# Twelve of 36 probability blocks per turn: transposed by VectorE and DMA in place of TensorE

## The chip, the cores and the metric

One Trainium2 chip, one core of it. The metric is the device time of one execution in microseconds (us). TensorE is PE in the profile, its weight loads PEld, VectorE is DVE, ScalarE is ACT, GpSimd is POOL, and SyncE, which issues most DMAs, is SP.

## The reference

One transformer block with two modulated layer norms. Batch 2, 1024 rows, 256 columns; 16 heads in 4 groups, each group with its own keys and values, head size 128.

```python
h = _layernorm(x) * (1 + ca) + sa
qkv = einsum('bsh,ph->bsp', h, weight_qkv)          # q: 4 heads, k: 1, v: 1, for each of 4 groups
scores = einsum('bsgqd,btgd->bgqst', q, k) * scale  # causal
attn = softmax(scores, axis=-1)
out = einsum('bgqst,btgd->bsgqd', attn, v)
x = x + ga * (out @ weight_proj.T)
h = _layernorm(x) * (1 + cb) + sb
x = x + gb * ffn(h)     # Hadamard transforms folded in, silu(gate) * up, down
```

## The kernel before

All products are made in three matmuls of split operands: a value is rounded to a high part (name ending in `_hi`) and the remainder is kept as a low part (`_lo`); `three` (L797) multiplies high by high, high by low and low by high.

The attention runs in 8 **turns**, one for each pair of batch and group. A turn first makes q, k and v (the steps "C" and "VT"), then goes over the 8 row blocks of 128 queries, from the last (row 7, 1024 keys) to the first (row 0, 128 keys). For row `i` and head `h` the step "S" makes the scores on PE (L903 to L909), DVE adds the mask and takes the row's maximum (L702), ACT takes the exponential and the row's sum (L487), and POOL inverts the sum and scales the row (L373, L378) into `prob`, in place. `prob` has two slots, so that the scores of row i-1 are made while row i is used.

A probability block (i, j) is 128 queries by 128 keys for 4 heads, so 128 x 512 numbers. There are 36 in a turn, numbered n = 0 to 35 in the order of `UNITS`: row 7 has n = 0 to 7, row 6 n = 8 to 14, row 5 n = 15 to 20, row 4 n = 21 to 25. Each must stand transposed for the product with v. The step "T" does so: PE transposes the 4 heads' 128 x 128 squares into one of two PSUM banks (L924, 4 matmuls against the identity), ACT copies the bank to `pt_hi` (L506), DVE subtracts to `pt_lo` (L706). The step "V" then multiplies block n by its v block (three matmuls of 512 columns) into the row's PSUM sum; it stands two blocks behind "T". When a row's last V is done, ACT and DVE split the row's output (`o_hi`, `o_lo`), and the step "Y" multiplies it by the projection weights (12 matmuls of 256 columns).

One list, `WALK`, made by `walk()` and written out by hand rules (`SCORES_AT` says after which block the next row's four S steps stand), sets the order of the steps of a turn. PE, ACT and DVE each go through this list and issue their own part of a step; all four engines run their instructions strictly in their written order, with semaphores between them. POOL has the four normalisations of each row in order of the rows, and after row 6 (`if s == 1`) it splits the next turn's q/k/v weights: `w_hi` (L331) and `w_lo` (L386). SP loads these weights from HBM, one load of `wp_raw` and one of `w_raw` a turn (L290, L294).

After the turns come the FFN's weight transforms and the FFN itself; the change touches them only in that the down weights `raw_down` and their sums and differences (`sum_dn`, `dif_dn`) are loaded and made at another time.

Of the kernel before, what the change touches and what calls it, by code (L numbers as in the profile page):

```python
# [5 lines left out]
F32 = mybir.dt.float32  # L6
F32R = mybir.dt.float32r
# [23 lines left out]
LAST = {i: max(n for n, u in enumerate(UNITS) if u[0] == i) for i in STEPS}  # L31

# [10 lines left out]
def walk():  # L43
# [24 lines left out]
    return out  # L68
# [21 lines left out]
def build(nc, x_in, wqkv, wproj, wmod, c_cols, wug, wdn, su_ug, su_dp, ws_ug, ws_dp, ident_in, mask_in, had_in, out):  # L90
    ctx = ExitStack()
    with ctx:
# [17 lines left out]
        pt_hi = sb("pt_hi", [P, 3, CH], F32R)  # L110
        pt_lo = sb("pt_lo", [P, 3, CH], F32R)
# [8 lines left out]
        raw_down = sb("raw_down", [P, NM * HID])  # L120
        sum_dn, dif_dn = (sb(name, [P, 2, KH, HID])[:, :, :, :] for name in ("sum_down", "dif_down"))
# [42 lines left out]
        raw_dn = raw_down[:, :].rearrange("p (a k o n) -> p a k o n", a=2, k=KH, o=2)  # L164
# [41 lines left out]
        pv_done, oh_done, ol_done = sem("pv_done"), sem("o_hi_done"), sem("o_lo_done")  # L206
        y_done, add_done = sem("y_done"), sem("x_added")
# [12 lines left out]
        PER_PE = {qkv_done: 12, vtr_done: 2, s_done: 32, t_done: NU, pv_done: NU, y_done: NT}  # L220
        PER_ACT = {qkv_hi: 10, vt_done: 2, v_hi_s: 2, exp_done: 32, pth_done: NU, oh_done: NT}
        PER_DVE = {qkv_lo: 10, v_lo_s: 2, max_done: 32, ptl_done: NU, ol_done: NT, add_done: NT}
        PER_POOL = {prob_done: 32, rinv_done: 32}
# [9 lines left out]
        CHUNKS += [("q", h, 1) for h in range(QPG)] + [("q", h, 0) for h in range(QPG)]  # L233

# [30 lines left out]
        def _(sp):  # L265
# [18 lines left out]
            sp.dma_start(raw_down[:, :], wdn).then_inc(raw_s[4], 16)  # L284
# [12 lines left out]
            wide = sum(i + 1 for i in STEPS if i >= CT)  # L297
# [10 lines left out]
        def _(pool):  # L308
# [39 lines left out]
            pool.wait_ge(raw_s[4], 16)  # L348
            a = raw_dn
            g_.tensor_tensor(sum_dn, a[:, :, :, 0, :], a[:, :, :, 1, :], ALU.add)  # L350
            g_.tensor_tensor(dif_dn, a[:, :, :, 0, :], a[:, :, :, 1, :], ALU.subtract).then_inc(fly_s, 1)
            pool.wait_ge(gate_ok, 1)
            for b in range(B):
                for g in range(NKV):
# [13 lines left out]
                    for s, i in enumerate(STEPS):  # L368
                        for h in range(QPG):
                            e = QPG * s + h  # L370

                            pool.wait_ge(exp_done, this(exp_done, t, e + 1))
                            g_.tensor_tensor(rinv[:, s % 2, h:h + 1], rsum[:, s % 2, h:h + 1], mone[:, :],  # L373
                                             ALU.pow).then_inc(rinv_done, 1)
                            pool.wait_ge(rinv_done, this(rinv_done, t, e + 1))
                            pool.sem_inc(pool_gate, 1)
                            row = prob[:, s % 2, h, 0:(i + 1) * P]
                            g_.tensor_scalar(row, row, rinv[:, s % 2, h:h + 1], 1.0, ALU.mult, ALU.mult).then_inc(prob_done, 1)  # L378
                        if s == 1:
# [7 lines left out]
                                             ALU.subtract).then_inc(w_ready, 1)  # L387

# [29 lines left out]
        def _(act):  # L418
# [37 lines left out]
            for b in range(B):  # L456
                for g in range(NKV):
# [34 lines left out]
                    for what, n, h in WALK:  # L492
# [72 lines left out]
        def _(dve):  # L565
# [96 lines left out]
            for b in range(B):  # L662
                for g in range(NKV):
# [21 lines left out]
                    for what, n, h in WALK:  # L685
# [390 lines left out]
```

## Time and profile before

| | |
|---|---|
| median of 3 runs | 979.47 us (979.19 to 979.89) |
| the profiled execution | 979.04 us |
| its span, first to last instruction | 977.2 us |
| mean granted TensorE clock | 0.997 |
| PE busy | 947.1 us |
| DVE busy | 653.1 us |
| ACT busy | 516.6 us |
| POOL busy | 467.7 us |

The span is shorter than the profiled execution's own time by 1.8 us. Busy times are of a single execution; matmuls are pipelined and their ends are modelled, so two starts in a row tell more of PE's pace than a duration does. A line number is that of the kernel before.

### The profile page before, as it was taken

The numbers are of one execution on the slowest core, as the hardware profiler recorded it, in microseconds if no ns is written. First come the engines' busy times: TensorE is split into PE (matmuls) and PEld (weight loads), VectorE is DVE, ScalarE is ACT, GpSimd is POOL, SyncE is SP. The second block draws the span as 40 slices with busy tenths as digits, with TensorE's granted clock in tenths as the row PEclk, the third lists the DMA queues.
The fourth block names the chain that finished last, engine by engine and source line by source line (L and its number), as shares of the span: only waits on it lengthen the run. The fifth ranks groups of instructions, "written<-read, shape, count | busy, mean of one in ns | idle before, by whom it ended". The sixth has DMA issues, their size and how long they took to land.

```text
span 977.2 us, 14506 instructions
## 1 busy us (share of the span) xinstructions
PE 947.1 (97%) x5344; PEld 816.0 (83%) x5344; DVE 653.1 (67%) x1290; ACT 516.6 (53%) x1085; POOL 467.7 (48%) x603
## 2 busy tenths in 40 slices
PE   6899999999999999999999999999999999999997
PEld 5688888888898889888988898889888987888885
DVE  6777657775777577757775777567757776864553
ACT  2466646664666466646664666466646665331221
POOL 3665646564556455545654565456545656120000
PEclk9999999999999999999999999999999999999999
DMA  8000000100010001000000010001000020000000
GB/s 313 24 1 33 2 22 1 33 1 22 1 33 2 22 1 33 1 23 1 33 1 22 1 33 1 22 1 34 1 1 1 1 87 1 1 8 15 21 21 21
DMA packets 9666, 21.92 MB, mean 22 GB/s; under 512 B 1280, under 2 KB 5504, under 8 KB 9472
## 3 DMA queue, kind: packets, MB, share of 16 engines
q1 hardware_dynamic: 8736, 20.45, 6.2%
q8 instruction: 40, 0.66, 0.3%
q10 hardware_dynamic: 864, 0.60, 0.2%
q14 instruction: 26, 0.21, 0.1%
HBM read 18.96 MB, written 2.10 MB: 22 GB/s over the span
## 4 chain that ended last, share of the span: by engine, by line
PE 80%; DVE 9%; ACT 5%; POOL 3%; issue 2%; DMA 1%; SPq 0%; DVEq 0%; POOLq 0%; ACTq 0%
PE ps L801 17%; PE ps L803 16%; PE ps L802 16%; PE ps L924 10%; PE ps L903 6%; PE ps L909 6%; PE ps L906 6%; ACT prob L487 2%; POOL rinv L373 2%; DVE pt_lo L706 2%; POOL prob L378 2%; DVE xhat L614 1%; DVE ps L702 1%; PE ps L825 1%; DVE v_lo L681 1%
## 5 line engine op out<-in xcount | busy, mean ns | idle before, releaser
L706 DVE TENSOR_TENSOR pt_lo<-ps,pt_hi 128x512 fp32r<-128x512 f32 x288 | 198.0, 690 | 101.7 <-ACT pt_hi L506 98.9
L506 ACT ACTIVATE pt_hi<-ps 128x512 fp32r<-128x512 f32 x288 | 171.0, 597 | 134.1 <-PE ps L924 132.6
L373 POOL TENSOR_TENSOR rinv<-rsum,mone 128x1 f32<-128x1 f32 x256 | 140.7, 550 | 211.5 <-ACT prob L487 210.7
L378 POOL TENSOR_SCALAR prob<-prob,rinv 128x1024 f32<-128x1024 f32 (+7 forms) x256 | 192.2, 751 | 53.3 <-POOL rinv L373 53.3
L487 ACT ACTIVATE prob<-ps,nmax 128x1024 f32<-128x1024 f32 (+7 forms) x256 | 189.5, 741 | 50.0 <-DVE nmax L702 48.3
L702 DVE CUSTOM_DVE_ANT_0 ps<-ps,mask_f 128x1024 f32<-128x1024 f32 (+7 forms) x256 | 192.9, 765 | 21.8 <-PE ps L909 19.5
L924 PE MATMUL ps<-ident,prob 128*128 128x128 f32 x1152 | 175.1, 273 | 6.2 <-DVE pt_lo L706 3.6
L924 PEld LDWEIGHTS ps<-ident,prob 128*128 128x128 f32 x1152 | 140.3, 140 | 36.8 <-DVE pt_lo L706 10.9
L801 PE MATMUL ps<-pt_hi,v_hi 128*128 128x512 f32 x288 | 132.5, 460 | 1.3 <-DVE pt_lo L706 0.5
L803 PE MATMUL ps<-pt_hi,v_lo 128*128 128x512 f32 x320 | 126.3, 395 | 0.0
L903 PE MATMUL ps<-k_hi,q_hi 128*128 128x512 f32 (+4 forms) x384 | 117.6, 360 | 0.0
L802 PE MATMUL ps<-pt_lo,v_hi 128*128 128x512 f32 x288 | 113.5, 394 | 0.0
L909 PE MATMUL ps<-k_hi,q_lo 128*128 128x512 f32 (+4 forms) x384 | 110.8, 343 | 0.0
L906 PE MATMUL ps<-k_lo,q_hi 128*128 128x512 f32 (+4 forms) x384 | 110.5, 342 | 0.0
L801 PE MATMUL ps<-h_hi,w_hi 128*128 128x512 f32 x192 | 76.1, 396 | 0.3 <-POOL h_lo L327 0.3
L906 PEld LDWEIGHTS ps<-k_lo,q_hi 128*128 128x128 f32 x384 | 71.0, 189 | 5.9
L903 PEld LDWEIGHTS ps<-k_hi,q_hi 128*128 128x128 f32 x384 | 68.1, 189 | 9.1
L802 PE MATMUL ps<-h_lo,w_hi 128*128 128x512 f32 x192 | 75.1, 391 | 0.0
L803 PE MATMUL ps<-h_hi,w_lo 128*128 128x512 f32 x192 | 75.0, 391 | 0.0
L909 PEld LDWEIGHTS ps<-k_hi,q_lo 128*128 128x128 f32 x384 | 70.7, 189 | 4.9
L801 PE MATMUL ps<-wp_hi,o_hi 128*128 128x256 f32 x256 | 73.8, 288 | 0.0
L803 PE MATMUL ps<-wp_hi,o_lo 128*128 128x256 f32 x256 | 72.2, 282 | 0.0
(134 smaller groups left out, 1575.8 us busy)
## 6 DMA issues: line engine op xcount, KB each, us to landing
w_raw<-in_wqkv SPq DMA_DIRECT2D x9, 768.0 KB, 4.2
wp_raw<-in_wproj SPq DMA_DIRECT2D x8, 512.0 KB, 3.5
x<-in_x SPq DMA_DIRECT2D x4, 512.0 KB, 9.8
prob<-in_wug SPq DMA_DIRECT2D x4, 512.0 KB, 5.3
out_y<-prob SPq DMA_DIRECT2D x4, 512.0 KB, 3.0
prob<-in_wmod SPq DMA_DIRECT2D x1, 1024.0 KB, 9.7
raw_down<-in_wdn SPq DMA_DIRECT2D x1, 1024.0 KB, 14.1
prob<-in_wmod SPq DMA_DIRECT2D x1, 512.0 KB, 5.2
```

The lines of the kernel that those rows point to most:

```text
L378: g_.tensor_scalar(row, row, rinv[:, s % 2, h:h + 1], 1.0, ALU.mult, ALU.mult).then_inc(prob_done, 1)
L487: a_.activation(prob[:, s % 2, h, 0:nb * w].rearrange("p (a n) -> p a n", a=nb), score_banks(i, h).rearrange("p (a n) -> p a n", a=nb)[:, ...
L506: a_.activation(pt_hi[:, n % 3, :], T[n % 2], ACT.Copy).then_inc(pth_done, 1)
L702: v_.tensor_tensor_reduce(row, row, late, -1.0, 3.0e38, ALU.add, ALU.min, nmax[:, s % 2, h:h + 1]).then_inc(max_done, 1)
L706: v_.tensor_tensor(pt_lo[:, n % 3, :], T[n % 2], pt_hi[:, n % 3, :].bitcast(F32), ALU.subtract).then_inc(ptl_done, 1)
L801: mm(dst, w_h, r_h, start=start, stop=False)
L802: mm(dst, w_h, r_l, start=False, stop=False)
L803: return mm(dst, w_l, r_h, start=False, stop=stop)
L903: mm(dst[:, a * CH:a * CH + wide], q_hi[:, h, q_at], k_hi[:, a * w:a * w + wide], start=True, stop=False)
L906: mm(dst[:, a * CH:a * CH + wide], q_hi[:, h, q_at], k_lo[:, a * w:a * w + wide], start=False, stop=False)
L909: last = mm(dst[:, a * CH:a * CH + wide], q_lo[:, h, q_at], k_hi[:, a * w:a * w + wide], start=False, stop=True)
L924: last = tr(T[n % 2][:, h * P:(h + 1) * P], prob[:, s % 2, h, j * P:(j + 1) * P], ident[:, :])
```

## The change

Blocks (i, j) with i in 7, 6, 5 and j among the row's last four leave PE: n = 4 to 7, 11 to 14 and 17 to 20, twelve of 36 ("swapped"; the other 24 are "turned").

For these, a new step "X" (row, head) has DVE transpose the 128 x 512 piece of `prob` in 32 x 32 squares into the buffer `blocks`, one instruction a head, four a row. When all four heads of a row are there, SP issues 16 transfers from SBUF to SBUF, each 32 partitions by 512 numbers, that put the squares in their places in one half of `swapped`. `blocks` is single: the next row's first X waits until these transfers have landed. X stands in the order where a count of assumed costs, begun at the step S, has reached 3300 (`BEHIND`).

The step "E" takes the place of "T" for these blocks: ACT copies the block from `swapped` to `pt_hi`, and POOL, not DVE, subtracts to `pt_lo`. PE has nothing to do in it. V then waits for POOL's semaphore.

POOL now goes through `WALK` too, for its S and E parts. The split of the next turn's weights moves from behind row 6's normalisations to behind the last one of row 4 (`WEIGHTS_AFTER = 4`). `pt_hi` and `pt_lo` get a fourth buffer. `raw_down` shares its space with `swapped`, and `sum_dn` and `dif_dn` with `blocks`, so that load and these two POOL operations move from the start of the program to the last turn.

```diff
+SWAP_ROWS = [7, 6, 5]
+GROUP = 4
+SWAPPED = [n for n, (i, j) in enumerate(UNITS) if i in SWAP_ROWS and j > i - GROUP]
+TURNED = [n for n in range(NU) if n not in SWAPPED]
...
+BEHIND = 3300
+WEIGHTS_AFTER = 4
+
+def with_blocks(walk):
+    cost = {"C": 1360, "VT": 900, "L": 1000, "T": 443, "V": 680, "Y": 1400, "E": 0}
+    out, open_blocks, now = [], [], 0
+    for what, n, h in walk:
+        while open_blocks and now >= open_blocks[0][0]:
+            out.append(open_blocks.pop(0)[1])
+        out.append((what, n, h))
+        now += 160 * (n + 1) if what == "S" else cost[what]
+        if what == "S" and n in SWAP_ROWS:
+            open_blocks.append((now + BEHIND, ("X", n, h)))
+    return out + [block for _, block in open_blocks]
...
+                    for r, i in enumerate(SWAP_ROWS):
+                        at = group(t, i)
+                        sp.wait_ge(block_done, this(block_done, t, QPG * (r + 1)))
+                        if at >= 2:
+                            sp.wait_ge(el_done, len(SWAPPED) + (at - 1) * GROUP)
+                        for kb in range(NB):
+                            for a in range(NB):
+                                sp.dma_start(swapped[kb * QB:(kb + 1) * QB, at % 2, a * GROUP * P:(a + 1) * GROUP * P],
+                                             blocks[a * QB:(a + 1) * QB, kb * GROUP * P:(kb + 1) * GROUP * P]).then_inc(swap_s[at % 2], 16)
...
+                    def swapped_low(n):
+                        pool.wait_ge(eh_done, this(eh_done, t, SWAPPED.index(n) + 1))
+                        g_.tensor_tensor(by_head(pt_lo, n), swapped_tile(t, n), by_head(pt_hi, n).bitcast(F32),
+                                         ALU.subtract).then_inc(el_done, 1)
+
+                    for what, i, h in WALK:
+                        if what == "E":
+                            swapped_low(i)
+                        if what == "S":
+                            normalise(i, h)
+                        if what == "S" and (i, h) == (WEIGHTS_AFTER, QPG - 1):
...
                             split_w()
...
+                        if t == TURNS - 1 and what == "S" and (i, h) == (2, QPG - 1):
+                            pool.wait_ge(raw_s[4], 16)
+                            g_.tensor_tensor(sum_dn, a[:, :, :, 0, :], a[:, :, :, 1, :], ALU.add)
+                            g_.tensor_tensor(dif_dn, a[:, :, :, 0, :], a[:, :, :, 1, :], ALU.subtract).then_inc(fly_s, 1)
...
+                        if what == "E":
+                            i, j = UNITS[n]
+                            if n >= 4:
+                                act.wait_ge(pv_done, this(pv_done, t, n - 3))
+                            if j == i - GROUP + 1:
+                                act.wait_ge(*landed(group(t, i)))
+                            a_.activation(by_head(pt_hi, n), swapped_tile(t, n), ACT.Copy).then_inc(eh_done, 1)
+                            exps()
...
+                        if what == "X":
+                            s = NT - 1 - n
+                            at = group(t, n)
+                            if h == 0 and at:
+                                dve.wait_ge(*landed(at - 1))
+                            dve.wait_ge(prob_done, this(prob_done, t, QPG * s + h + 1))
+                            v_.transpose(blocks[:, :].rearrange("p (k j h q) -> p j k h q", k=NB, j=GROUP, h=QPG)[:, :, :, h, :],
+                                         prob[:, s % 2, h, (n + 1 - GROUP) * P:(n + 1) * P].rearrange(
+                                             "p (j k q) -> p j k q", j=GROUP, k=NB)).then_inc(block_done, 1)
...
+                            if n in SWAPPED:
+                                pe.wait_ge(el_done, this(el_done, t, SWAPPED.index(n) + 1))
+                            else:
+                                pe.wait_ge(ptl_done, this(ptl_done, t, turned(n) + 1))
```

How it moves the order, at three places. The first is **DVE in the first turn, around row 6's scores**: the `pt_lo` of n = 1 to n = 3, with the maxima (two rows each, `ps,nmax` and `nmax`) of scores (6,1), (6,2) and (6,3). Before:

```order
L706 TENSOR_TENSOR pt_lo<-ps,pt_hi 128x512 [waits pt_hi_done]
L702 ISA ps,nmax<-ps,mask_f 128x2x448 [waits scores_done]
L702 ISA nmax 128x1
L706 TENSOR_TENSOR pt_lo<-ps,pt_hi 128x512 [waits pt_hi_done] x3
L702 ISA ps,nmax<-ps,mask_f 128x2x448 [waits scores_done]
L702 ISA nmax 128x1
```

Now:

```order
L795 TENSOR_TENSOR pt_lo<-ps,pt_hi 128x512 [waits pt_hi_done]
L803 STREAM_TRANSPOSE blocks<-prob 128x4x4x32 [waits prob_done,blocks_swapped0]
L791 ISA ps,nmax<-ps,mask_f 128x2x448 [waits scores_done]
L791 ISA nmax 128x1
L795 TENSOR_TENSOR pt_lo<-ps,pt_hi 128x512 [waits pt_hi_done] x2
L803 STREAM_TRANSPOSE blocks<-prob 128x4x4x32 [waits prob_done]
L791 ISA ps,nmax<-ps,mask_f 128x2x448 [waits scores_done]
L791 ISA nmax 128x1
```

The first of these transposes is X (6,0). It waits for row 7's transfers, and it stands ahead of the maximum of (6,2) and of the low parts of n = 2 and 3. The low part of n = 4 is gone from DVE.

The second place is **POOL in the first turn, behind the third normalisation of row 4**. Before, the weights' split stands behind row 6's last normalisation:

```order
L373 TENSOR_TENSOR rinv<-rsum,mone 128x1 [waits exp_done]
L378 TENSOR_SCALAR prob<-prob,rinv 128x896 [waits rinv_done]
L331 TENSOR_SCALAR w_hi<-w_raw 128x1536 [waits w_raw_loaded,qkv_done]
L386 TENSOR_TENSOR w_lo<-w_raw,w_hi 128x1536 [waits pool_self]
L373 TENSOR_TENSOR rinv<-rsum,mone 128x1 [waits exp_done]
```

Now it stands behind row 4's last, among the low parts of row 5:

```order
L448 TENSOR_TENSOR pt_lo<-swapped,pt_hi 128x512 [waits swapped_hi_done]
L438 TENSOR_TENSOR rinv<-rsum,mone 128x1 [waits exp_done]
L443 TENSOR_SCALAR prob<-prob,rinv 128x640 [waits rinv_done]
L398 TENSOR_SCALAR w_hi<-w_raw 128x1536 [waits w_raw_loaded,qkv_done]
L463 TENSOR_TENSOR w_lo<-w_raw,w_hi 128x1536 [waits pool_self]
L448 TENSOR_TENSOR pt_lo<-swapped,pt_hi 128x512 [waits swapped_hi_done] x3
```

The first `pt_lo` is that of n = 17, the three at the end are those of n = 18, 19 and 20; between them stand the normalisation of (4,3) and the whole split.

The third place is **SP in the first turn**. It issued two weight loads a turn; now 48 transfers follow them:

```order
L345 DMA wp_raw<-in_wproj 128x1024 [waits wp_ready]
L349 DMA w_raw<-in_wqkv 128x1536 [waits w_ready]
L359 DMA swapped<-blocks 32x512 [waits blocks_turned]
L359 DMA swapped<-blocks 32x512 x15
L359 DMA swapped<-blocks 32x512 [waits blocks_turned]
L359 DMA swapped<-blocks 32x512 x15
```

## Rows read from the trace of the kernel before

**Rows 1.** The page: busy time, share of the span and instructions of each engine.

```profile
PE 947.1 (97%) x5344; PEld 816.0 (83%) x5344; DVE 653.1 (67%) x1290; ACT 516.6 (53%) x1085; POOL 467.7 (48%) x603
```

**Rows 2.** Groups of instructions: busy us, mean ns of one, idle before.

```profile
L706 DVE TENSOR_TENSOR pt_lo<-ps,pt_hi 128x512 fp32r<-128x512 f32 x288 | 198.0, 690 | 101.7 <-ACT pt_hi L506 98.9
L924 PE MATMUL ps<-ident,prob 128*128 128x128 f32 x1152 | 175.1, 273 | 6.2 <-DVE pt_lo L706 3.6 <-POOL prob L378 2.3
L506 ACT ACTIVATE pt_hi<-ps 128x512 fp32r<-128x512 f32 x288 | 171.0, 597 | 134.1 <-PE ps L924 132.6
...
L386 POOL TENSOR_TENSOR w_lo<-w_raw,w_hi 128x1536 fp32r<-128x1536 f32 x8 | 28.1, 3507 | 0.7
...
L327 POOL TENSOR_TENSOR h_lo<-h,h_hi 128x512 fp32r<-128x512 f32 x14 | 18.2, 1301 | 39.5 <-ACT h_hi L446 23.6 <-DVE h_hi L622 15.8
...
L331 POOL TENSOR_SCALAR w_hi<-w_raw 128x1536 fp32r<-128x1536 f32 x9 | 13.3, 1482 | 1.3 <-DMA w_raw<-in_wqkv 1.3
```

**Rows 3.** Timeline of PE, second turn: start, duration, instruction, idle before.

```profile
174.70 0.28 PE L801 MATMUL ps<-wp_hi,o_hi 128*128 128x256 f32 x1
...
176.14 0.60 PE L924 MATMUL ps<-ident,prob 128*128 128x128 f32 x4
...
177.28 0.60 PE L924 MATMUL ps<-ident,prob 128*128 128x128 f32 x4
...
193.13 0.40 PE L801 MATMUL ps<-pt_hi,v_hi 128*128 128x512 f32 x1
...
193.83 0.60 PE L924 MATMUL ps<-ident,prob 128*128 128x128 f32 x4
```

**Rows 4.** Timeline of POOL, DVE and ACT, second turn: (6,3) is normalised, (4,3) too.

```profile
162.22 1.09 DVE L702 CUSTOM_DVE_ANT_0 ps<-ps,mask_f 128x896 f32<-128x896 f32 x1
...
163.71 1.00 ACT L487 ACTIVATE prob<-ps,nmax 128x896 f32<-128x896 f32 x1
...
164.89 0.55 POOL L373 TENSOR_TENSOR rinv<-rsum,mone 128x1 f32<-128x1 f32 x1 [2.42 <-ACT prob L487]
...
165.64 1.02 POOL L378 TENSOR_SCALAR prob<-prob,rinv 128x896 f32<-128x896 f32 x1 [0.20 <-POOL rinv L373]
...
189.32 0.80 POOL L378 TENSOR_SCALAR prob<-prob,rinv 128x640 f32<-128x640 f32 x1 [0.21 <-POOL rinv L373]
```

**Rows 5.** Timeline of PE, second turn: the steps at which the three places begin and end.

```profile
165.98 0.51 PE L903 MATMUL ps<-k_hi,q_hi 128*128 128x384 f32 x2
...
167.03 0.60 PE L924 MATMUL ps<-ident,prob 128*128 128x128 f32 x4
...
179.55 0.45 PE L903 MATMUL ps<-k_hi,q_hi 128*128 128x320 f32 x2
...
186.47 0.60 PE L924 MATMUL ps<-ident,prob 128*128 128x128 f32 x4
...
191.31 0.39 PE L903 MATMUL ps<-k_hi,q_hi 128*128 128x512 f32 x1
```

**Rows 6.** Timeline of SP's queue, then DMA issues with the us from issue to landing.

```profile
137.60 0.33 SPq L290 DMA_DIRECT2D wp_raw<-in_wproj  x1
...
793.57 2.59 SPq L300 DMA_DIRECT2D prob<-in_wug  x4
...
wp_raw<-in_wproj SPq DMA_DIRECT2D x8, 512.0 KB, 3.5
...
sc<-in_c SPq DMA_DIRECT2D x1, 2.0 KB, 1.7
```

**Rows 7.** Timeline of DVE, second turn: maximum of (6,0) ends, low part of n = 1.

```profile
153.76 0.14 DVE L702 DVE_READ_ACCUMULATOR2_ANT nmax<- 128x1 f32 x1
...
157.61 0.69 DVE L706 TENSOR_TENSOR pt_lo<-ps,pt_hi 128x512 fp32r<-128x512 f32 x1
```

**Rows 8.** PE's longest wait in a turn; stages with busy us and granted clock (PEclk).

```profile
37.86 0.63 PE L825 MATMUL ps<-ident,xhat 128*128 128x128 f32 x4 [3.72 <-DVE xhat L614]
...
38.60:42.00 3.40, 3.40 (x9) 2.63 (x9) 1.18 (x2) 1.93 (x4) 3.32 (x3) 0.50 0.01 2
```

More of the change, by code:

```diff
@@ L67, in walk @@
     out += [("V", NU - 3, 0), ("V", NU - 2, 0), ("T", NU - 1, 0), ("Y", 2, 0), ("V", NU - 1, 0), ("Y", 1, 0), ("Y", 0, 0)]
-    return out
+    return with_blocks([("E", n, 0) if what == "T" and n in SWAPPED else (what, n, h) for what, n, h in out])
+BEHIND = 3300
[11 more added lines that the diff above has]
+    return out + [block for _, block in open_blocks]
 WALK = walk()
@@ L109, in build @@
         prob = sb("prob", [P, 2, QPG, SEQ])
-        pt_hi = sb("pt_hi", [P, 3, CH], F32R)
-        pt_lo = sb("pt_lo", [P, 3, CH], F32R)
+        pt_hi = sb("pt_hi", [P, 4, CH], F32R)
+        pt_lo = sb("pt_lo", [P, 4, CH], F32R)
+        blocks = sb("blocks", [P, GROUP * CH])
+        swapped = sb("swapped", [P, 2, GROUP * CH])
+        raw_down = swapped[:, 0, :]
+        sum_dn, dif_dn = (blocks[:, n * 4 * HID:(n + 1) * 4 * HID].rearrange("p (a k n) -> p a k n", a=2, k=KH)
+                          for n in range(2))
         o_hi = sb("o_hi", [P, 2, CH], F32R)
@@ L206, in build @@
         pv_done, oh_done, ol_done = sem("pv_done"), sem("o_hi_done"), sem("o_lo_done")
+        block_done, swap_s = sem("blocks_turned"), [sem(f"blocks_swapped{n}") for n in range(2)]
+        eh_done, el_done = sem("swapped_hi_done"), sem("swapped_lo_done")
         y_done, add_done = sem("y_done"), sem("x_added")
@@ L295, in _ @@
                                  wqkv[bass.ds(g + 1, 1), :, :].rearrange("a p (k n) -> p (a k) n", k=KH)).then_inc(wraw_s, 16)
-            wide = sum(i + 1 for i in STEPS if i >= CT)
+                    for r, i in enumerate(SWAP_ROWS):
[7 more added lines that the diff above has]
+                                             blocks[a * QB:(a + 1) * QB, kb * GROUP * P:(kb + 1) * GROUP * P]).then_inc(swap_s[at % 2], 16)
+            sp.wait_ge(el_done, (TURNS + 1) * len(SWAPPED))
+            sp.dma_start(raw_down, wdn).then_inc(raw_s[4], 16)
+            wide = len([n for n in TURNED if UNITS[n][0] >= CT])
             sp.wait_ge(t_done, this(t_done, TURNS - 1, wide))
@@ L367, in _, with normalise @@
                     ln_low(1, b, g, 0)
[L368 to L379, printed above, removed]
+                    def normalise(i, h):
+                        s = NT - 1 - i
+                        e = QPG * s + h
+                        pool.wait_ge(exp_done, this(exp_done, t, e + 1))
+                        g_.tensor_tensor(rinv[:, s % 2, h:h + 1], rsum[:, s % 2, h:h + 1], mone[:, :],
+                                         ALU.pow).then_inc(rinv_done, 1)
+                        pool.wait_ge(rinv_done, this(rinv_done, t, e + 1))
+                        pool.sem_inc(pool_gate, 1)
+                        row = prob[:, s % 2, h, 0:(i + 1) * P]
+                        g_.tensor_scalar(row, row, rinv[:, s % 2, h:h + 1], 1.0, ALU.mult, ALU.mult).then_inc(prob_done, 1)
+                    def swapped_low(n):
[8 more added lines that the diff above has]
+                        if what == "S" and (i, h) == (WEIGHTS_AFTER, QPG - 1):
                             pool.wait_ge(wraw_s, (t + 2) * 16)
```

53 lines of the change are left out of this document (31 added, 22 removed).

## The prediction

> **What bounds the kernel now.** I read the page first: PE is busy for 947.1 of 977.2 us, the next engine, DVE, for 653.1 [rows 1]. PE sets the time, and its waits are small: in front of its 1152 transposes it idled 6.2 us in all [rows 2]. Then I read PE's starts, since durations overlap. Y, T and T follow at 174.70, 176.14 and 177.28 [rows 3]: a Y takes 1.44 us, and a T with the V behind it 1.14 us. A V without a T in front takes 0.70 us, from 193.13 to 193.83 [rows 3]. So a T costs PE 0.44 us, part of it in the matmul behind it. Third come the chains from a score to its normalised row and from there to a low part, since the change puts V behind them [rows 4, 7].
>
> **What is removed.** 12 T in each of 8 turns: 96 x 0.44 = 42 us of PE's time, 5.3 us a turn. This is the whole gain, and it needs PE to find its operands ready.
>
> **What is added off PE.** DVE loses 12 low parts a turn (690 ns) and gets 12 transposes of the same 128x512. No row shows such a transpose; I take 0.7 us by the nearest, the low part itself [rows 2], and twice that as the far end, nothing below. ACT's copy now reads SBUF and stays at 0.6 us. Neither engine is full. POOL gets 12 low parts a turn, 1.30 us each by the `h_lo` of the same size [rows 2]. On its sum of 467.7 us that is 125 us more [rows 1], which fits; its place in the order does not. PE without T's consumes a V each 0.70 us, POOL makes a low part each 1.3 us, and POOL runs strictly in order, so that each low part stands behind the normalisation and the split written ahead of it.
>
> The fourth buffer costs nothing. The later load of `raw_down`, and its two POOL operations behind row 2 of the last turn, lie beside PE's rows 2 to 0; if that cover fails they cost two 1.3 to 3.5 us operations once [rows 2]. SP's two weight loads are not late behind the transfers: they are wanted only a turn later.
>
> **The transfers.** SP's steady issue takes 0.33 us, four other loads in a row took 2.59 us, so 0.65 each [rows 6]. A landing takes 1.7 us for 2 KB and 3.5 us for 512 KB. The transfers of a row are 16, of 64 KB. I take 15 x 0.33 + 2.0 = **7.0 us** from DVE's last transpose of a row to the landing (the short issue, since a transfer has 32 lines). Ends: 4 us, if issue hardly counts and the 1 MB moves like the 512 KB load; 15 x 0.65 + 3.5 = 13 us. The Trainium skill, page "DMA: Bandwidth & Descriptors", section "Anatomy of one DMA — SWDGE (gpsimd) path", gives for another issue path 2.0 us fixed plus the bytes at 436 GB/s. As an estimate by that page one 1 MB transfer would take 4.4 us, and the sum below would come to about 1115. No run here shows a transfer from SBUF to SBUF.
>
> **Place 1, row 7's swapped blocks (second turn's clock).** The last transpose of row 7 starts when DVE is done with the maximum of (6,0), at 153.90 [rows 7], ends at 154.6, and the data land at 161.6. DVE reaches X (6,0) at 158.3, behind the low part of n = 1 [rows 7], and waits until 161.6. Behind it are queued: X itself (162.3), the maximum of (6,2), 1.15 us (163.45), the low part of n = 2 (164.15). ACT's exponential of (6,2) then ends at 164.6, the copy of n = 3 at 165.2; DVE: low part of n = 3 at 165.9, X (6,1) 166.6, maximum of (6,3) 167.75. ACT ends its exponential at 168.9, POOL the inversion and scaling (164.89 to 166.66, so 1.8 us [rows 4]) at 170.7, and the low part of n = 5, which stands behind it, at 172.0. V of n = 5 starts then and ends at 172.7. Before, the step behind it started at 165.98 [rows 5]. Loss 6.7 us, with the four T already out.
>
> **Place 2, row 6.** From 172.7: S (5,0) 1.2 to its end by the starts of [rows 5] and the tail of the last matmul, maximum 1.0, X (6,3) 0.7, at 175.65; landing at 182.65; X (5,0) 183.35; the low part of row 7's output, queued behind it, 184.05; Y of row 7 (1.44) ends 185.5, having waited 2.9. DVE meanwhile: low part of n = 10 at 184.75, X (5,1) 185.45, maximum of (5,3) 186.45; exponential 187.5, normalisation 189.2, low part of n = 11 190.5, of n = 12 191.8. V of n = 12 ends at 192.5; before, S (4,0) started at 179.55 [rows 5]. Loss 12.95 in all, so 6.3 here.
>
> **Place 3, row 5 and the weights.** From S (4,0) to the end of S (4,3) took 6.92 us [rows 5], now 0.44 less: 199.0. Scaling of (4,3) ended 3.65 us behind that point (186.47 to 190.12 [rows 4, 5]); POOL, which first has the low part of n = 17, comes to 203.65. Then the split: 1.48 + 3.51 + a gap, 5.06 us [rows 2], to 208.7, and the low part of n = 18 at 210.0. PE's work in between is V 16, Y, V 17, 2.84 us. V of n = 18 ends at 210.7, after a wait of 7 us; before, 191.31 [rows 5]. Loss 19.4 in all, so 6.4 here. Behind it POOL's low parts of n = 19 and 20 keep pace with the S steps between.
>
> **The clock.** After PE's wait of 3.72 us the granted clock was 0.50 (1.2 GHz) for 3.4 us of full work [rows 8], which loses 1.7 us. Two waits a turn are longer than that one. Behind n = 18 I count 1.7, behind n = 11 only 1.1, since the V of n = 12 waits 0.6 anyway: 2.8 us a turn. The Trainium skill, page "TensorE: Matmul & The Clock Gate", section "Part 1: The HAM clock gate", says that the throttled state is the default and activity lifts it; by that, the trace agrees. Without it the sum would be 22 us less, 1134.
>
> **Sum.** 8 x (6.7 + 6.3 + 6.4 + 2.8) = 8 x 22.2 = 178. Against the profiled execution's own time, 979.04 + 178 = **1157 us**; it stands 0.4 below the median of the runs, which is nothing here. A microsecond of landing time moves places 1 and 2 by one each, 16 us in the sum.
>
> **Rivals.**
> 1. *The transfers are quick, POOL alone is in the way.* With nothing lost on DVE: POOL's chain from (6,3) makes n = 5 late by 1.7 us net, n = 12 by 1.4, n = 18 by 5.9 (190.12 + 5.06 + 1.30 + 0.70 = 197.2 against 191.31). 8 x 9.0 = 72, so 1051. With a landing of 3.7 us and the transposes still queued on DVE, 1157 - 16 x 3.3 = 1104. For it: transfers of a free queue. Against: 16 issues. Chance 0.22.
> 2. *Faster.* The low parts are ready whenever PE comes, and the 42 us are kept: 979 - 42 = 937. It decides at n = 18: S to low part must take less than PE's 2.84 us, where the rows add to 10.0 (3.65 + 5.06 + 1.30). For it speaks only that POOL, ACT and DVE all have idle time; chance 0.03.
> 3. *The transfers are slow.* Landing 13 us: 1157 + 16 x 6 = 1253, for it the 0.65 us issue. Chance 0.10.
> 4. *The matmuls that leave are hidden anyway, nothing waits*: about 979. The starts show T on PE's own path [rows 3], so 0.01.
>
> The Trainium skill, page "VectorE: DVE Perf Modes", section "Rules for kernel authors", advises TensorE for 128x128 transposes where a PSUM destination will do; it gives no time for a mix as here, and it points the way of my forecast.
>
> **How the numbers follow.** My forecast, a time set by all three places, has 0.64; with landing 4 to 10 us it runs from 1109 to 1205, a transpose of twice the time adds some 10. The range 1080 to 1215 takes that and the upper half of rival 1, and leaves out its lower half, rivals 2, 3 and 4: 0.2 or a little more. A measurement of this kernel tells 0.2% from no change. Faster 0.03, same 0.01, slower 0.96.
>
> **What would show it.** In the changed kernel's profile: PE's busy time lower but waits in front of Y and the V matmuls of some 25 us a turn, the longest, about 7 us, on POOL's `pt_lo` and eight times; DVE's transposes of X (6,0) and X (5,0) waiting some 3 us each on a DMA; a granted clock well under 0.997; turns some 22 us longer. Wrong would be: landing far from 7 us, the wait at n = 18 under 5 us, or low parts far from 1.3 us.

## The result and the profile after

The changed kernel takes **1258.59 us** (median of 4 runs, 1257.09 to 1261.66) against 979.33 us of the kernel before (4 runs, 978.55 to 979.89): 1.2856 times as long, 95% interval 1.283 to 1.2882. The forecast was 1157 us with a range of 1080 to 1215. The direction was right, the time lies 44 us above the range, at rival 3 (1253 us).

The page of the changed kernel: the busy line, two of its groups and two of its DMA issues.

```profile
PE 993.4 (79%) x4960; PEld 827.5 (66%) x4960; DVE 639.0 (51%) x1290; ACT 514.5 (41%) x1085; POOL 585.8 (47%) x699
...
L803 DVE STREAM_TRANSPOSE blocks<-prob 128x512 f32<-128x512 f32 x96 | 67.7, 705 | 137.3 <-DMA swapped<-blocks 125.9
...
L448 POOL TENSOR_TENSOR pt_lo<-swapped,pt_hi 128x512 fp32r<-128x512 f32 x96 | 119.6, 1271 | 0.0
...
swapped<-blocks SPq DMA_DIRECT2D x384, 64.0 KB, 2.0
...
wp_raw<-in_wproj SPq DMA_DIRECT2D x8, 512.0 KB, 3.8
```

PE has 384 transposes fewer and is yet busy for 46 us longer than before [rows 1], at a mean granted clock of 0.875. DVE's transpose takes 0.705 us (0.7 taken), POOL's low part 1.27 us (1.30 taken), and a single transfer lands in 2.0 us (as taken). None of the new operations is dearer than in the sum. What they wait for is: PE's largest waits, then those of DVE and of ACT on the transfers (us in total, times, the longest).

```profile
PE ps L899 <- POOL pt_lo L448: 118.2, 41, 6.7
PE ps L899 <- DVE pt_lo L795: 61.8, 13, 8.3
PE ps L899 <- DVE o_lo L809: 55.3, 8, 7.4
...
DVE blocks L803 <- DMA swapped<-blocks: 125.9, 16, 8.6
...
ACT pt_hi L595 <- DMA swapped<-blocks: 71.2, 16, 6.9
```

DVE's 16 waits are two a turn, of 7.9 us each, where about 3 was expected. One turn (the fourth), from its timelines: SP's queue behind row 7's last transpose; DVE's last transpose of row 7, and the first of row 6 and of row 5; PE's seven waits.

```profile
452.91 10.01 SPq L359 DMA_DIRECT2D swapped<-blocks  x16
```

```profile
452.18 0.71 DVE L803 STREAM_TRANSPOSE blocks<-prob 128x512 f32<-128x512 f32 x1
...
464.35 0.71 DVE L803 STREAM_TRANSPOSE blocks<-prob 128x512 f32<-128x512 f32 x1 [7.63 <-DMA swapped<-blocks]
...
490.93 0.71 DVE L803 STREAM_TRANSPOSE blocks<-prob 128x512 f32<-128x512 f32 x1 [8.26 <-DMA swapped<-blocks]
```

```profile
466.71 0.80 PE L899 MATMUL ps<-pt_hi,v_hi 128*128 128x512 f32 x1 [7.35 <-DVE pt_lo L795]
470.38 0.79 PE L899 MATMUL ps<-pt_hi,v_hi 128*128 128x512 f32 x1 [0.23 <-POOL pt_lo L448]
474.36 0.79 PE L899 MATMUL ps<-pt_hi,v_hi 128*128 128x512 f32 x1 [2.34 <-POOL pt_lo L448]
492.37 0.55 PE L899 MATMUL ps<-wp_hi,o_hi 128*128 128x256 f32 x1 [7.36 <-DVE o_lo L809]
498.40 0.79 PE L899 MATMUL ps<-pt_hi,v_hi 128*128 128x512 f32 x1 [1.85 <-POOL pt_lo L448]
513.72 0.50 PE L899 MATMUL ps<-pt_hi,v_hi 128*128 128x512 f32 x1 [3.74 <-POOL pt_lo L448]
521.39 0.79 PE L899 MATMUL ps<-pt_hi,v_hi 128*128 128x512 f32 x1 [6.71 <-POOL pt_lo L448]
```

The 16 issues of one row take 10.01 us, 0.63 each, not 0.33. DVE's transpose ends at 452.89 and the next one can start at 464.35: **the landing is 11.5 us behind, not 7.0**. It is so in most turns; in some rows one of the 16 issues is long (up to 1.57 us), and the landing is then up to 12.4 us behind. Everything that stands behind the waiting transpose on DVE comes late: the low part of n = 2 (PE waits 7.35 at 466.71, place 1) and the low part of row 7's output (7.36 at 492.37, in front of Y, place 2). At 521.39 stands the wait for the low part of n = 18, place 3, 6.71 us where 7 was forecast. The POOL timeline in front of it shows the split of the weights in its way, as forecast:

```profile
513.63 0.54 POOL L438 TENSOR_TENSOR rinv<-rsum,mone 128x1 f32<-128x1 f32 x1
514.38 0.80 POOL L443 TENSOR_SCALAR prob<-prob,rinv 128x640 f32<-128x640 f32 x1 [0.21 <-POOL rinv L438]
515.14 1.47 POOL L398 TENSOR_SCALAR w_hi<-w_raw 128x1536 fp32r<-128x1536 f32 x1
516.70 3.42 POOL L463 TENSOR_TENSOR w_lo<-w_raw,w_hi 128x1536 fp32r<-128x1536 f32 x1
520.08 3.72 POOL L448 TENSOR_TENSOR pt_lo<-swapped,pt_hi 128x512 fp32r<-128x512 f32 x3
```

The table of windows of the same turn (PE busy, PEld, DVE, ACT, POOL, granted clock, DMA share, GB/s) shows the clock at its lower level behind each of the long waits:

```profile
458.00:464.00 6.00, 1.36 (x7) 0.91 (x5) 0.00 (x0) 0.00 (x0) 1.02 (x1) 0.98 0.43 105
464.00:476.00 12.00, 6.58 (x13) 3.84 (x14) 5.23 (x9) 4.76 (x9) 7.28 (x8) 0.50 0.00 0
...
488.00:500.00 12.00, 5.78 (x19) 4.59 (x20) 5.12 (x9) 3.29 (x6) 4.34 (x5) 0.50 0.14 34
...
516.00:524.00 8.00, 2.61 (x6) 2.04 (x7) 0.00 (x0) 0.00 (x0) 7.71 (x5) 0.50 0.30 100
```

In the row 458 to 464 PE, DVE and ACT all stand nearly still while the transfers run at 105 GB/s.

### The profile page after: what moved, and what is told of

It reads as the page before. It is cut to its first block, busy times and chain, and to the rows that moved or that the text cites. A ratio compares the mean times of both kernels' runs of the same rounds, so it can differ in the third digit from the quotient of the medians.

```text
span 1255.3 us, 14290 instructions
## 1 busy us (share of the span) xinstructions
PE 993.4 (79%) x4960; PEld 827.5 (66%) x4960; DVE 639.0 (51%) x1290; ACT 514.5 (41%) x1085; POOL 585.8 (47%) x699
## 4 chain that ended last, share of the span: by engine, by line
PE 43%; SPq 17%; DVE 12%; POOL 12%; ACT 6%; DMA 4%; issue 4%; POOLq 0%; DVEq 0%; ACTq 0%
SPq L359 17%; PE ps L899 11%; PE ps L901 10%; PE ps L900 10%; DMA swapped<-blocks 4%; POOL prob L443 4%; DVE ps L791 3%; PE ps L1023 3%; ACT prob L568 3%; PE ps L1001 3%; DVE blocks L803 3%; PE ps L1004 3%; PE ps L1007 3%; POOL rinv L438 3%; POOL pt_lo L448 2%
## 5 line engine op out<-in xcount | busy, mean ns | idle before, releaser
L899 PE MATMUL ps<-pt_hi,v_hi 128*128 128x512 f32 x288 | 149.6, 519 | 181.8 <-POOL pt_lo L448 118.2
L587 ACT ACTIVATE pt_hi<-ps 128x512 fp32r<-128x512 f32 x192 | 114.4, 596 | 245.2 <-PE ps L1023 243.7
L899 PEld LDWEIGHTS ps<-pt_hi,v_hi 128*128 128x128 f32 x288 | 61.9, 215 | 223.0 <-POOL pt_lo L448 144.1
L795 DVE TENSOR_TENSOR pt_lo<-ps,pt_hi 128x512 fp32r<-128x512 f32 x192 | 132.0, 688 | 76.4 <-ACT pt_hi L587 75.5
L803 DVE STREAM_TRANSPOSE blocks<-prob 128x512 f32<-128x512 f32 x96 | 67.7, 705 | 137.3 <-DMA swapped<-blocks 125.9
L1023 PE MATMUL ps<-ident,prob 128*128 128x128 f32 x768 | 123.7, 284 | 4.7 <-POOL prob L443 4.3
L448 POOL TENSOR_TENSOR pt_lo<-swapped,pt_hi 128x512 fp32r<-128x512 f32 x96 | 119.6, 1271 | 0.0
L1023 PEld LDWEIGHTS ps<-ident,prob 128*128 128x128 f32 x768 | 99.3, 147 | 26.2 <-POOL prob L443 6.6
L899 PEld LDWEIGHTS ps<-wp_hi,o_hi 128*128 128x128 f32 x256 | 52.6, 205 | 62.0 <-issue 58.6
L595 ACT ACTIVATE pt_hi<-swapped 128x512 fp32r<-128x512 f32 x96 | 56.3, 623 | 72.2 <-DMA swapped<-blocks 71.2
```

Source lines behind the costliest of these rows:

```text
L899: mm(dst, w_h, r_h, start=start, stop=False)
L1023: last = tr(T[m % 2][:, h * P:(h + 1) * P], prob[:, s % 2, h, j * P:(j + 1) * P], ident[:, :])
```

## The experiments

The theory after the result: two causes, the transfers' issue time on SP and POOL's place in the order, overlap in each turn, and the slow clock comes on top. The rivals: it is the bytes and not the issues that take the time; the transposes on DVE are in the way even without transfers; the clock alone is most of it. Where no number of runs is given, a time is of one execution; the kernel before, run on the same chips, had medians of 978.65 to 979.38 us.

### Without transfers, and with fewer

In `e1_no_transfers` DVE writes its squares straight into `swapped`, SP transfers nothing, and ACT waits for DVE. It leaves out the placing of the squares, as all runs with 0, 4 or 8 transfers a row do; these tell times only.

```diff
-                        for kb in range(NB):
-                            for a in range(NB):
-                                sp.dma_start(swapped[...], blocks[...]).then_inc(swap_s[at % 2], 16)
...
-                                act.wait_ge(*landed(group(t, i)))
+                                act.wait_ge(block_done, this(block_done, t, QPG * (SWAP_ROWS.index(i) + 1)))
...
-                            v_.transpose(blocks[:, :]...
+                            v_.transpose(swapped[:, at % 2, :]...
```

> Leaves out the placing of the 32x32 squares: DVE writes them straight into the buffer that ACT and POOL read, so nothing waits for a DMA. Theory A (the transfers' issue sets two of the three places): the two waits on landed squares go, the POOL waits stay; 1060 to 1110 us, PE waits in front of V only on POOL, granted clock above 0.93. Theory B (POOL's place in the order alone does it, the transfers only overlap its delay): little changes, above 1200 us. Theory C (the transposes on DVE are what is late): no change either, with waits on DVE's pt_lo as long as now.

Measured 1104.08 us, clock 0.944. 155 of the 279 us are gone with the transfers. DVE waits on no transfer, and PE's long waits are all on POOL (on the low parts of DVE it waits 6.6 us, never more than 0.8 at a time):

```profile
PE ps L889 <- POOL pt_lo L438: 119.3, 48, 6.7
```

The other two move the same 1 MB a row in 4 transfers of 128 x 512 numbers, and in 8 of 32 x 1024:

```diff
-                            for a in range(NB):
-                                sp.dma_start(swapped[kb * QB:(kb + 1) * QB, ...
+                            sp.dma_start(swapped[:, at % 2, kb * GROUP * P:(kb + 1) * GROUP * P],
+                                         blocks[:, kb * GROUP * P:(kb + 1) * GROUP * P]).then_inc(swap_s[at % 2], 16)
```

```diff
-                            for a in range(NB):
+                            for a in range(2):
+                                sp.dma_start(swapped[kb * QB:(kb + 1) * QB, at % 2, a * 2 * GROUP * P:(a + 1) * 2 * GROUP * P], ...
```

> The same bytes a row in 4 transfers of 128x512 instead of 16 of 32x512, squares not placed. Theory A1 (each issue in a burst costs SP about 0.6 us whatever it moves): 4 issues in 2.5 us, landing 4.5 to 5.5 us behind DVE's last transpose instead of 11.5, time 1120 to 1160 us. Theory A2 (the rate of about 100 GB/s while they run is a limit of moving SBUF to SBUF): landing stays near 11 us, time near 1259.

> The same bytes a row in 8 transfers of 32x1024, each inside one quarter of the partitions, squares not placed. Theory A1: 8 issues in 5 us, landing at 6.5 to 7.5 us, time 1165 to 1195 us, half way between four and sixteen transfers. Theory A2: landing near 11 us, 1259 us. If a quarter of the partitions is slow by itself: longer issues, landing above 8 us.

Measured 1124.72 and 1165.78 us. SP's issues of the kernel with 4 and of the one with 8 transfers a row (duration in ns, min/median/max):

```profile
L358 SPq DMA_DIRECT2D swapped<-blocks x96: 465/603/617, 53.3 to 904.2; - x96
...
DMA to landing us min/median/max: 2.3/2.5/4.8
```

```profile
L359 SPq DMA_DIRECT2D swapped<-blocks x192: 507/591/1829, 50.5 to 947.7; - x192
...
DMA to landing us min/median/max: 2.2/2.4/4.9
```

An issue takes 0.59 to 0.60 us for 64, 128 or 256 KB: it is priced by the transfer, not by the byte, and the landing behind it grows by only 0.5 us from 64 to 256 KB. From 0 over 4 and 8 to 16 transfers the time goes 1104, 1125, 1166, 1259. With the same bytes, 134 of the 155 us come with the transfers beyond four, so the number of issues is the cause and the bytes are not. By the forecast's rule of 16 us for a microsecond of landing, 8 issues more (4.8 us) should give 77, and 93 were measured.

### POOL's place

`e4_weights_later` sets one number, so that the split of the weights stands behind row 3's normalisations; `e5_no_transfers_weights_later` does so without transfers.

```diff
-WEIGHTS_AFTER = 4
+WEIGHTS_AFTER = 3
```

> The changed kernel with the split of the next weights behind row 3's last normalisation instead of row 4's. Theory A: the wait of 6.7 us in front of V of block 18 falls by about 5 us in each of 8 turns, and with it one fall of the clock; 1259 - 8 x 5 to 7 = 1203 to 1219 us. Rival: the 5 us come back at the start of row 2, whose normalisations then stand behind the split: 1250 to 1259 us.

> No transfers (squares not placed) and the weights' split behind row 3. Theory A (the costs of the transfers and of POOL's order add up): the wait of 6.7 us in front of block 18's V falls by 5 us and the clock stays up behind it, so 1104 - 8 x 5 to 6.7 = 1050 to 1064 us; what is left are the waits on POOL's low parts behind the normalisations of (6,3) and (5,3), 5 to 7 us a turn. Rival (the split only covers another delay): above 1090 us.

Measured 1222.8 (36 us less) and 1069.25 (35 less), both a little above what was expected. The longest wait on POOL fell from 6.7 to 4.1 and to 3.0 us. So the move won 4.5 us a turn, of the 5.0 that the split lasts.

`e6_low_on_dve` is the last one with the low parts of the swapped blocks on DVE as well, and `e9_transfers_low_on_dve` the same with all transfers.

```diff
-                        if what == "E":
-                            swapped_low(i)
...
+                        if what == "E":
+                            dve.wait_ge(eh_done, this(eh_done, t, SWAPPED.index(n) + 1))
+                            v_.tensor_tensor(by_head(pt_lo, n), swapped_tile(t, n), by_head(pt_hi, n).bitcast(F32),
+                                             ALU.subtract).then_inc(el_done, 1)
```

> As the run before, and the low parts of the swapped blocks made by DVE, as before the change, in place of POOL. Squares not placed. Theory A (what is left are POOL's low parts behind its normalisations): PE has no long waits, time is 979 - 42 = 937 us plus what DVE's 12 transposes a turn queue in front of its low parts, so 940 to 960 us, granted clock 0.99 or more. Rival (DVE becomes the bound with 12 transposes and 36 low parts a turn): 965 to 1000 us, waits of PE on DVE.

> The changed kernel with all its transfers, the low parts of swapped blocks on DVE and the weights' split behind row 3: POOL's part of the cost taken out, the transfers left in. Together with the runs without transfers it completes a table of two by two. If the two causes add: 971 + (1259 - 1104) = 1126 us. If POOL's delays lie partly behind the landings: the transfers alone cost more than that, 1150 to 1190 us, with waits of 7 us in front of V of block 2 and of row 7's Y, and 3 to 4 us at block 17.

Measured 971.27 and 1162.14 us. The page of `e6_low_on_dve`:

```profile
PE 919.4 (95%) x4960; PEld 776.9 (80%) x4960; DVE 692.8 (71%) x1386; ACT 513.4 (53%) x1085; POOL 488.0 (50%) x603
```

It expected 940 to 960: PE's busy time fell by 27.7 us, not by 42, and its idle time rose by 20 (969.5 - 919.4 = 50.1 against 30.1), with 15.3 and 6.0 us in waits on low parts of DVE, which stand behind its transposes. That is what the rival of DVE's transposes is worth here. The other 14 us of the 42 are explained only in part: a V behind a wait takes 0.81 us to the next start (159.29 to 160.10), like one behind a T (0.78), and not the 0.70 of the forecast; for 33 such waits that is some 3 us, an estimate. The rest is open.

Four runs together, against 971 with neither cause: POOL alone (the low parts there, the split early, `e1_no_transfers`) 133 us, the transfers alone (`e9_transfers_low_on_dve`) 191, both 287 and not 324. So some 36 us of the two delays overlap. The clock alone can't be most of it: PE's whole work in the changed kernel is 74 us longer than in `e6_low_on_dve` (993.4 against 919.4 us, the same matmuls), and that is the most that the slow clock can have cost.

### One row alone

`e7_row7_only` swaps only the blocks of row 7 (`SWAP_ROWS = [7]`).

> The changed kernel with row 7's four blocks alone swapped, 32 of 36 by TensorE. Only place 1 is left: no second row queues behind the buffer, so X (6,0) does not exist and DVE doesn't wait; only ACT waits at block 4 for the landing, about 11.5 us behind the last transpose of row 7. Split of the weights behind row 4, where no low part stands behind it now. Theory A: landing at about 166.1 on the clock of the turn described, block 4's low part at 168.0 where PE comes at 162 to 164, so a wait of 4 to 6 us a turn, and a gain of 1.7: 979 + 8 x 2.5 to 5.5 (with clock) = 999 to 1023 us. Rival (a single group has slack enough): under 979 us.

Measured 1045.09 us, above the expected range. A third of the gain is bought with a quarter of the loss. PE's waits in one turn, and the windows around:

```profile
388.26 0.79 PE L899 MATMUL ps<-pt_hi,v_hi 128*128 128x512 f32 x1 [5.73 <-POOL pt_lo L448]
391.49 0.79 PE L899 MATMUL ps<-pt_hi,v_hi 128*128 128x512 f32 x1 [1.59 <-POOL pt_lo L448]
```

```profile
384.00:395.00 11.00, 5.15 (x13) 3.95 (x14) 0.00 (x0) 3.17 (x6) 6.50 (x6) 0.55 0.24 66
395.00:400.00 5.00, 5.00 (x32) 4.63 (x31) 4.10 (x7) 3.28 (x7) 1.98 (x3) 0.97 0.00 0
```

The two waits are 7.3 us a turn; less 1.8 for four T that makes 44 of the 66 us lost. The rest, 2.7 us a turn, is the size of what PE's work at the lower clock from 388 to 395 costs.

### The clock by itself

`e8_pe_kept_busy` puts 24 matmuls of no use in front of V of n = 2 and of n = 18, so that PE works where it waited.

```diff
+                            if n == 2:
+                                pe.wait_ge(qkv_lo, this(qkv_lo, t, 10))
+                            if n == 18:
+                                pe.wait_ge(add_done, this(add_done, t, 2))
+                            for _ in range({2: 24, 18: 24}.get(n, 0)):
+                                mm(X[1], q_hi[:, 0, 0:P], k_hi[:, 0:CH], start=True, stop=True)
```

> The changed kernel with 24 extra matmuls of 512 columns, whose result nobody reads, in front of V of block 2 and of block 18, about 5 us of work each under waits of 7.3 and 6.7 us. Theory A (each long wait also costs the fall of the clock behind it): clock stays at 1.0 behind these two, 1259 - 8 x 1.7 to 3.4 = 1232 to 1245 us, mean granted clock above 0.92. Rival (the slow stretches lie under other waits and cost nothing): 1255 to 1262 us with a higher clock all the same.

Measured 1251.78 us. In front of n = 2 the filler was too short to keep PE working up to the low part:

```profile
456.06 5.63 PE L1043 MATMUL ps<-k_hi,q_hi 128*128 128x512 f32 x24
464.68 0.50 PE L899 MATMUL ps<-pt_hi,v_hi 128*128 128x512 f32 x1 [2.99 <-DVE pt_lo L795]
466.47 0.79 PE L899 MATMUL ps<-pt_hi,v_hi 128*128 128x512 f32 x1 [0.68 <-DVE pt_lo L795]
```

The wait went on for 2.99 us, and from the second V behind it the clock is at its lower level again (0.79 in place of 0.50 us). In front of n = 18 it was long enough. The filler, V of n = 18 without a wait, V of n = 19, and a window over them; then the same two V in the changed kernel:

```profile
514.12 6.79 PE L1043 MATMUL ps<-k_hi,q_hi 128*128 128x512 f32 x24
520.75 0.41 PE L899 MATMUL ps<-pt_hi,v_hi 128*128 128x512 f32 x1
...
523.30 0.39 PE L899 MATMUL ps<-pt_hi,v_hi 128*128 128x512 f32 x1
...
519.00:523.00 4.00, 4.00 (x21) 3.23 (x20) 0.63 (x2) 0.20 (x1) 4.00 (x4) 1.00 0.59 195
```

```profile
521.39 0.79 PE L899 MATMUL ps<-pt_hi,v_hi 128*128 128x512 f32 x1 [6.71 <-POOL pt_lo L448]
...
525.78 0.39 PE L899 MATMUL ps<-pt_hi,v_hi 128*128 128x512 f32 x1
```

Here the granted clock stays at 1.00, and from V of n = 18 to V of n = 19 PE takes 2.55 us in place of 4.39. Over the eight turns it is 2.5 to 2.7 (once with a wait of 1.3 us ahead of V) in place of 4.3 to 4.9, so **the fall of the clock behind place 3 costs 2.0 us a turn**, 16 in all. In the total only 7 us were won where 14 to 27 had been expected: other stretches became longer, rows of issues among them (up to 11.4 us for 16, in place of 10.0). So the run gives the clock's cost at place 3, and not at the other two.

### Looking for a version that pays

Row 6's blocks are far from where they are wanted, so I tried it alone: `b1_row6_direct` has only row 6, the low parts on DVE, the split back behind row 6, and the 16 transfers. `b2_row6_dram` has 8 writes of 128 KB to HBM and 2 reads of 512 KB in their place, and `b3_row6_dram_placed` moves DVE's four transposes by hand to where it had idle time.

```diff
-SWAP_ROWS = [7, 6, 5]
+SWAP_ROWS = [6]
-WEIGHTS_AFTER = 4
+WEIGHTS_AFTER = 6
...
+                                sp.dma_start(scratch[:, :, a, u, :].rearrange("k q n -> q k n"),
+                                             pair(blocks[a * QB:(a + 1) * QB, :])[:, u, :, :]).then_inc(out_w[u], 16)
...
+                            sp.dma_start(swapped[:, at % 2, :].rearrange("p (a u n) -> p a u n", a=NB, u=2)[:, :, u, :],
+                                         scratch[:, :, :, u, :].rearrange("k q a n -> (k q) a n")).then_inc(swap_s[at % 2], 16)
...
+    for h, before in enumerate([("T", 4, 0), ("V", 3, 0), ("V", 4, 0), ("S", 5, 0)]):
+        out.insert(out.index(before), ("X", 6, h))
```

(The first hunk is of the first kernel, the next two of the second, the last of the third.)

> Row 6's four blocks alone swapped, low parts on DVE, weights' split back behind row 6, 16 transfers from SP. Row 6 has the longest way from its normalisation to its last blocks: on the clock of the turn described X (6,3) ends at 166.7, the squares land at 178.2, V of block 11 is wanted at 176.4 and has its low part at 179.5. Landing theory: a wait of about 3 us, gain 1.7: 979 + 8 x 1.4 = 985 to 998 us. Rival (a single row fits): 965 to 972 us.

> As the run before, but the squares go through a buffer in HBM: 8 writes, four of them behind the first two heads, and 2 reads, so that only 4 issues, a write's landing and a read stand behind the last transpose. Landing theory: about 8.5 us instead of 11.5, block 11's low part at 176.5 where PE comes at 176.4: no wait; 979 - 8 x 1.7 = 965 us at best, 965 to 976 with DVE's transposes in front of its low parts. Rival (writes to HBM and reading back take 11 us or more): 985 us and more.

> The run through HBM with DVE's four transposes moved in its order: X (6,0) behind V of block 1, X (6,1) and X (6,2) into the gaps behind the low parts of blocks 5 and 6, X (6,3) right ahead of S (5,0), so that none stands in front of a low part that PE waits for at once. Waits in front of T of 0.86 us should go; landing about 1 us later than before relative to V of block 11. Theory (only the queue on DVE eats the gain): 970 to 977 us. Rival (the transfer stays what counts): 980 to 986 us.

Measured: 1031.3; 983.59 (4 runs, 982.64 to 985.58; 1.0047 times before, 1.003 to 1.0063); 983.0 (8 runs, 977.86 to 986.42; 1.0036 times, 1.0016 to 1.0056). All three miss what was hoped for. In the first, SP's queue and the one long wait of a turn:

```profile
382.96 11.21 SPq L359 DMA_DIRECT2D swapped<-blocks  x16
```

```profile
397.07 0.79 PE L895 MATMUL ps<-pt_hi,v_hi 128*128 128x512 f32 x1 [4.93 <-DVE pt_lo L791]
```

From the end of the last transpose to ACT's copy it is 12.7 us there (382.93 to 395.66), the longest of the eight turns (11.6 to 12.7; the shortest have 10.01 us of issues, as in the changed kernel). With the way through HBM, whose first half of the writes starts when two of the four heads are there, it is 8.3 us in the same turn, and 7.5 to 9.0 over the eight. PE's waits of this second kernel:

```profile
PE ps L1025 <- DVE pt_lo L793: 9.7, 16, 0.9
...
PE ps L901 <- DVE pt_lo L797: 6.8, 12, 1.2
```

The long wait is gone, but these two have come to 16.5 us where the same two were 4.1 before, and of the gain of four T a turn, 14 us by the forecast's price, PE's busy time shows 8.2 (938.9 against 947.1). By hand-placing, 0.6 us more was won, less than the scatter of these runs: the waits in front of T fell from 9.7 to 3.6 us, those in front of V rose from 6.8 to 9.1, so that the time came out in the range of the rival. **No whole version here is faster than the kernel before.**

`b4_row6_direct_busy` is the first of these with PE kept working for the clock's sake: before V of n = 11 it waits for DVE's sum of row 7 and then makes 20 matmuls of no use.

```diff
+                            if n == 11:
+                                pe.wait_ge(add_done, this(add_done, t, 1))
+                                for _ in range(20):
+                                    mm(X[0], q_hi[:, 0, 0:P], k_hi[:, 0:CH], start=True, stop=True)
```

> Row 6 alone with direct transfers (1031 us, one wait of 4.9 us a turn and a granted clock of 0.50 for some 5 us behind it), with 20 extra matmuls of 512 columns in front of the waiting V of block 11, about 4.3 us of work under the wait; nobody reads their result. Theory (the fall of the clock costs as much as the slow stretch shows): clock stays at 1.00, 1031 - 8 x 2 to 3 = 1007 to 1015 us. Rival (the fall lies beside other work): 1029 to 1033 us with the clock at 1.00 all the same.

Measured 1062.04 us. The wait I gave the filler was itself the long one, since DVE's sum stands behind the low part that waits for the transfers:

```profile
PE ps L1037 <- DVE x L811: 36.2, 8, 5.2
```

So the filler came behind the wait and not in its place, and the run tells nothing of the clock.

## Why the prediction was wrong in its size

Its schedule of a turn can be laid beside the trace. I set the two time scales against each other at the start of row 7's last transpose, 153.90 in the forecast and 452.18 here, 298.3 apart:

| start of | forecast | seen | later by |
|---|---|---|---|
| V of n = 5 | 172.0 | 176.1 | 4.1 |
| Y of row 7 | 184.05 | 194.1 | 10.0 |
| V of n = 11 | 190.5 | 200.1 | 9.6 |
| V of n = 18 | 210.0 | 223.1 | 13.1 |

**The step that failed first is "15 x 0.33 + 2.0 = 7.0 us".** The 2.0 was right. The 0.33 is SP's issue when it stands alone [rows 6]; in a row of them it is 0.59 to 0.63, which the same group of rows had shown (2.59 us for four). I had kept that as the far end and took the short one for a reason that no row bore out, that a transfer has 32 lines. Landing 11.5 is 4.5 more, at place 1 and at place 2: 8 x 9.0 = 72 us, 1229 in all. The places, their queues and what each held up were right: V of n = 5 comes 4.1 later, and of the 5.9 by which Y comes later still 4.5 are the second landing.

**The second is place 3, which I took as free of the landing.** With 7.0 it would have been. With 11.5 the data of row 5 come at 509.39, and on ACT the exponentials of (4,2) and (4,3) stand behind the copy of n = 17 that waits for them:

```profile
509.39 0.63 ACT L595 ACTIVATE pt_hi<-swapped 128x512 fp32r<-128x512 f32 x1 [2.47 <-DMA swapped<-blocks]
509.93 0.78 ACT L568 ACTIVATE prob<-ps,nmax 128x640 f32<-128x640 f32 x1
```

PE's scores of (4,3) end (507.69) 0.8 us later than the 9.6 account for (the lower clock), and POOL's scaling of (4,3), at 515.18, 2.8 us later than that, against the 203.65 of the forecast. So 3.6 us more lateness is made between n = 11 and n = 18; the table has 3.5. The wait at n = 18 then has the forecast size, 6.71 for 7.

**The third is the clock behind place 1, a term that was put at nothing.** The sum had 2.8 us a turn, behind n = 18 and n = 11 only. But behind the wait at n = 2 the clock is at its lower level until row 5's first scores are made: from V of n = 5 (474.36) to the T behind S (5,0) (477.60) PE takes 3.24 us, where the steps of [rows 3, 5] take 0.70 + 1.05. These 1.5 us stand ahead of row 6's last transposes, so Y and n = 11 come later by them. Behind n = 11 it is 0.8 (1.1 taken), behind n = 18 some 1.6 in this turn and 2.0 over all by `e8_pe_kept_busy` (1.7 taken): 3.9 to 4.3 us a turn on the path, for 2.8. PE's work itself grew by more, 9.2 us a turn against `e6_low_on_dve`, and most of that then lies in front of other waits; this division is worked out from one turn, and an experiment showed it at place 3 alone. In `e7_row7_only` and `b1_row6_direct`, where one long wait stands alone in a turn, PE's busy time is 959.6 and 957.1 us against 938.9 in `b2_row6_dram`, with as many matmuls: 2.6 and 2.3 us a turn.

The sum again, for this turn: 19.4 that the forecast had up to n = 18, 13.1 of the table, and 1.6 of the clock behind it are 34.1, and the turn is 34.1 us longer than before (132.9 against 98.75). It is the quickest of the seven whole turns. Their mean is 134.0 us, 35.1 more than before, and 979 + 8 x 35.1 = 1260, for 1259 measured.

The rule can be tried apart from the landing's size. With four and with eight transfers the last one landed 4.4 and 6.8 us behind the transpose in most turns; by 16 us for each microsecond the forecast would have said 1115 and 1154 there, and 1125 and 1166 were measured. It is 10 and 12 us low there, and 30 at 11.5 us, where place 3 comes in.

**What held**: PE's loss stands in three places, on DVE twice and on POOL once; the durations of the transpose, the low part and the split; "a microsecond of landing, 16 us" up to where place 3 comes in; faster only if low parts were ready when PE came, which no whole version reached. Of its signs one was false: PE's busy time is not lower but 46 us higher, since the matmuls behind the waits run at the lower clock. **Rival 3** gave 1253 for a landing of 13 us, at 0.10. It was the right mechanism, though its nearness to 1259 is in part luck: 1.5 of its microseconds (24 us) were not there, and place 3 and the clock made up for them. **Rival 1's** 1104 for quick transfers agrees with `e1_no_transfers` in number only: it was reckoned with a landing of 3.7 us, the kernel has none, and its 1051 for that case is 53 us short. PE waits there on POOL 6.7 us and five times 0.3 to 3.0 us a turn; how the 53 us divide among these small waits, the clock and the gain that did not come was not worked out. **The gain**, 42 us, was too high: `e6_low_on_dve` has 27.7 us less PE work, 0.29 for a T and not 0.44, and `b2_row6_dram` 8.2 for 32 T, 0.26. The 1115 us that the forecast had estimated by the Trainium skill, page "DMA: Bandwidth & Descriptors", section "Anatomy of one DMA — SWDGE (gpsimd) path", is for one transfer of 1 MB a row; `e2_four_transfers`, with four, landed 4.4 us behind and comes to 1125, which does not speak against it, but the change has sixteen, and their issues are what that estimate leaves out. The advice of the Trainium skill, page "VectorE: DVE Perf Modes", section "Rules for kernel authors", to leave 128x128 transposes to TensorE where PSUM can take them, agrees with every whole version here: none is faster than the kernel before (979.33 us; the nearest is 983.0).

## What to carry to other kernels

A transfer in a row of many costs its issue time on the queue; where a row of the trace shows the issue both alone and in a burst, take the burst's, and count issues before bytes. When one landing is held back, ask of every place that you called free whether it stays free at the far end of the range: here a bound of 13 us would have drawn the third place in. Work that leaves the bounding engine must have its operands ready before that engine comes by; 0.3 us saved for each of four to twelve blocks is lost by one wait of 5 us in a turn, and the lower clock behind it adds 2 us or more.

## What the runs showed of the hardware that I had not expected

SP's issue of an SBUF-to-SBUF transfer took 0.59 to 0.60 us in the median, in a row of 16, 8 or 4, whatever the size from 64 to 256 KB, with a single one of 1.1 to 1.6 us in some rows; the load of `raw_down`, alone, took 0.33 us to issue. One of 64 KB landed in 2.0 us, of 128 KB in 2.4, of 256 KB in 2.5; eight writes of squares to HBM and two reads back were there sooner than 16 direct ones (7.5 to 9.0 against 11.6 to 12.7 us from the last transpose to ACT's copy). Behind waits of 5 to 7 us the granted clock stayed at 0.50 (1.2 GHz) for 12 us where further waits followed (464 to 476) and for 7 in `e7_row7_only` (388 to 395), and for some 5 us where PE then worked without a break (397 to 402 in `b1_row6_direct`).
